# Stage orders of five engines rewritten: the first late tiles join the hand-written part, and each sort is cut in two

## The reference, cut to what matters

```
# block 1, for each of 4 batches, on layernorm(x): w1 is [512, 512], w2 is [512, 256]
def smooth_quant_linear(x, w):            # int8-like product, smoothed per column
    s  = sqrt(colmax|x| / colmax|w|)      # floors left out
    xs, ws = x / s, w * s
    x_q = round(xs / (rowmax|xs| / 127));  w_q = round(ws / (rowmax|ws| / 127))
    return x_q @ w_q.T * x_scale * w_scale.T
gate, up = split(smooth_quant_linear(x, w1));  a = silu(gate) * up
x1 = x + smooth_quant_linear(a, w2)
# block 2, on layernorm(x1): 8 experts, the best 2 of each token
weights = softmax over the best 2 of (xn @ router_w)
out = x1 + sum over the 2 experts of weight * (silu(xn @ gate_w) * (xn @ up_w)) @ down_w
```

## Time and profile before

| | us |
|---|---|
| runs of the kernel before: median (lowest to highest) | 386.32 (385.65 to 386.40) |
| the profiled execution | 386.07 |
| its span on the core | 384.2 |
| PE busy | 324.4 |
| POOL busy | 244.4 |
| DVE busy | 222.9 |
| ACT busy | 205.3 |

### The profile page before, as it was taken

How to read it: one execution, slowest core, us unless ns; L and a number is a source line. 1 busy time by engine, 2 the same in 40 slices (tenths; PEclk the granted TensorE clock), 3 DMA queues, 4 the chain that set the end, 5 groups by cost and what they waited for, 6 DMA issues and landing times.

```text
span 384.2 us, 6264 instructions
## 1 busy us (share of the span) xinstructions
PE 324.4 (84%) x1863; PEld 192.2 (50%) x1863; DVE 222.9 (58%) x511; ACT 205.3 (53%) x386; POOL 244.4 (64%) x271
## 2 busy tenths in 40 slices
PE   4697877867888876589889897999999999999980
PEld 2354535535656743385565444555555555555530
DVE  3585887889897988868577822333333333333320
ACT  1649838969987696138644333444444444444430
POOL 6484697889999961584572163556667756665441
PEclk9999989999998999989999999999999999999997
DMA  8773807654593337146344354556687666775543
GB/s 248 252 296 100 317 21 262 199 196 143 214 341 125 88 133 265 38 164 171 159 141 166 52 142 77 100 101 117 124 137 122 123 92 121 126 133 94 101 56 55
DMA packets 27552, 56.80 MB, mean 148 GB/s; under 512 B 2624, under 2 KB 13888, under 8 KB 25600
## 3 DMA queue, kind: packets, MB, share of 16 engines
q0 software_dynamic: 8736, 20.45, 29.2%
q1 hardware_dynamic: 17968, 35.39, 26.8%
q10 hardware_dynamic: 816, 0.54, 0.5%
HBM read 37.50 MB, written 18.87 MB: 147 GB/s over the span
## 4 chain that ended last, share of the span: by engine, by line
PE 45%; issue 14%; DVE 13%; POOL 13%; ACT 8%; DMA 3%; POOLq 2%; SPq 0%; DVEq 0%; ACTq 0%
PE bank_h L1306 18%; PE bank_q L1327 9%; PE bank_t L1291 3%; DVE amax L717 3%; PE bank_q L1172 3%; PE bank_q L1223 2%; DVE rmax L747 2%; ACT w_in L1027 2%; POOL out L678 2%; PE bank_h L1200 2%; DVE packed L870 2%; POOL x L639 2%; PE bank_t L1172 2%; POOL w_in L657 2%; PE bank_q L1212 2%
## 5 line engine op out<-in xcount | busy, mean ns | idle before, releaser
L1306 PE MATMUL bank_h<-gu_hi,xT 128*128 x312 | 104.0, 379 | 1.6 <-DVE xT L953 1.6
L1306 PE MATMUL bank_h<-gu_lo,xT 128*128 x156 | 59.2, 380 | 0.0
L953 DVE SCALAR_TENSOR_TENSOR xT<-bank_t,xT 128x512 f16<-128x512 f32 x39 | 26.8, 689 | 53.0 <-ACT xT L1085 53.0
L1327 PE MATMUL bank_q<-dn_hi,aT 128*128 x156 | 52.7, 380 | 3.2 <-DVE aT L971 2.9
L1306 PEld LDWEIGHTS bank_h<-gu_hi,xT 128*128 128x128 f16 x312 | 30.5, 98 | 31.0 <-issue 1.9
L657 POOL DMA_INDIRECT w_in<-tokens,gather_at x30 | 29.9, 995 | 22.8 <-PE bank_t L1291 10.8
L575 POOL TENSOR_TENSOR gu_lo<-stage,gu_hi 128x1024 bf16<-128x1024 f32 x16 | 34.0, 2135 | 9.7 <-ACT gu_hi L1042 9.5
L717 DVE TENSOR_REDUCE amax<-bank_t 128x1 f32<-128x512 f32 x48 | 30.9, 684 | 6.9 <-PE bank_t L1172 5.2
L678 POOL DMA_INDIRECT out<-h,scatter_at x17 | 26.9, 1580 | 12.1 <-ACT h L1114 5.5
L1092 ACT ACTIVATE gated<-bank_h 128x256 f32<-128x256 f32 x39 | 14.9, 383 | 36.0 <-PE bank_h L1306 33.4
L961 DVE SCALAR_TENSOR_TENSOR gated<-bank_h,gated 128x256 f32<-128x256 f32 x39 | 16.5, 422 | 30.2 <-ACT gated L1092 30.2
(11 more groups left out here) (196 smaller groups left out, 716.9 us busy)
## 6 DMA issues: line engine op xcount, KB each, us to landing
stage<-in_L_ffn_gate_proj SPq DMA_DIRECT2D x8, 512.0 KB, 4.8
stage<-in_L_ffn_up_proj SPq DMA_DIRECT2D x8, 512.0 KB, 6.2
stage<-in_L_ffn_down_proj SPq DMA_DIRECT2D x8, 512.0 KB, 5.0
x<-in_x SPq DMA_DIRECT2D x4, 1024.0 KB, 6.8
out<-x SPq DMA_DIRECT2D x4, 1024.0 KB, 4.2
tokens<-xn SPq DMA_DIRECT2D x4, 1024.0 KB, 5.4
x_in<-in_x SPq DMA_DIRECT2D x3, 1024.0 KB, 6.4
w_in<-in_fside_BxS2xS SPq DMA_DIRECT2D x3, 1024.0 KB, 5.4
```

Source lines behind the costliest of these rows:

```text
L953: dve.scalar_tensor_tensor(out=xT[i % 2][:, 1].rearrange("p c t -> p (c t)"), in0=bank, scalar=X_SCALE, in1=xT[i % 2][:, 0].rearrange("p c ...
L1306: ins = pe.matmul(bank, xT[i % 2][:, part, c], rhs[:, cols], start=(c == 0 and m == 0), stop=(c == C - 1 and m == 2))
L1327: ins = pe.matmul(bank, aT[i % 2][:, part, c], rhs[:, cols], start=(c == 0 and n == 0), stop=(c == FC - 1 and n == 2))
```

## The change

It has four parts.

1. All five lists are rewritten. They hold the same stages, apart from the new ones named below, in another order.
2. The lists in the text now reach further: `FIRST = 11`. The loop appends tiles from 11 on, and late tiles 9 and 10 stand in the lists among early tiles 6 to 9. In the lists of PE, DVE and ACT the loop's pattern is unchanged; POOL's loop still starts at tile 9 and is the same.
3. The stage `table` on PE is cut in two: `sort` runs all steps of a group but the last, `table` the last. Between them other stages may stand. For group 0 they stand next to each other; for group 1 `scores 7` is between them, for group 2 `a low 4`.
4. `FILLERS` has other numbers: 103 in place of 100. Seven now stand ahead of `rows 1 3`, seven in place of three ahead of `rows 1 1`, three ahead of `place 0`; the six ahead of `w1 transposed 1` and the five of sort step 0 are gone.

The semaphores of gathers get names of their own for early and late tiles; what they wait for is the same.

```
+FIRST = 11
-    "w1 scale row 0, high 4, normalise 1 1, high 5, silu 0, high 6, high 7, high 8, rows 1 1, rows 2 0, x up 1, "
+    "x transposed 0, high 4, high 5, normalise 1 1, silu 0, high 6, rows 1 1, high 7, rows 2 0, high 8, high 9, "
-    ("w1 columns", 0): 9, ("x columns", 0): 4, ("rows 1", 0): 2, ("w1 scale row", 0): 30, ("rows 1", 1): 3,
-    ("rows 2 inverse", 0): 18, ("w1 transposed", 1): 6, ("rows 1", 2): 6, ("product 2", 0): 8, ("sort step", 0): 5,
-    ("sort step", 1): 3, ("sort step", 2): 3, ("sort step", 3): 3,
+    ("w1 columns", 0): 9, ("x columns", 0): 4, ("rows 1", 0): 2, ("w1 scale row", 0): 28, ("rows 1", 1): 7,
+    ("rows 2 inverse", 0): 20, ("rows 1", 2): 2, ("product 2", 0): 10, ("x columns", 3): 2, ("rows 1", 3): 7,
+    ("place", 0): 3, ("sort step", 1): 3, ("sort step", 2): 3, ("sort step", 3): 3,
...
-        act_order.append(("x high", EARLY))
-        dve_order.append(("x low", EARLY))
+        act_order.append(("x high", FIRST))
+        dve_order.append(("x low", FIRST))
         for i in range(EARLY, TILES):
             if i + J < TILES:
                 pool_order.append(("gather", i + J))
...
-            if i >= EARLY + 2:
-                act_order.append(("take y", i - 2))
+        for i in range(FIRST, TILES):
+            act_order.append(("take y", i - 2))
...
+            pe_order += [("up first", i), ("a low", i - 1), ("up rest", i), ("take y", i - 1)]
+            act_order += [("a high", i - 1), ("gate", i)]
+            dve_order += [("a low", i - 1), ("up", i)]
...
-            def sort(g):
-
-                bank = ring_w.fill(pe, "table", 0, g)
+            def sort(part, g):
+
                 steps = K * len(GROUPS[g])
-                for n in range(steps):
+                bank = ring_w.fill(pe, "sort", 0, g) if part == 0 else ring_w.bank(ring_w.before("sort", 0, g))
+                for n in range(steps - 1) if part == 0 else (steps - 1,):
...
+                     "sort": partial(sort, 0), "table": partial(sort, 1),
```

44 lines of the change are left out of this document (19 added, 25 removed), and 97 rows, old and new, of tables (ACT_ORDER, DVE_ORDER, PE_ORDER, POOL_ORDER).

## The result

| | before | changed |
|---|---|---|
| median of the runs on one chip | 386.36 us (4 runs, 385.65 to 386.91) | 394.33 us (4 runs, 393.4 to 394.56) |
| ratio, 95% interval | | 1.0204 (1.0175 to 1.0232) |
| profiled execution | 386.07 us, span 384.2 | 394.46 us, span 392.6 |
| mean granted clock of PE | 0.980 | 0.966 |

What follows compares the result with a forecast made beforehand. PE was taken as the bound, its late loop already tight at 4.54 us per tile, so only the loop's start could move. Seven terms summed to -4.6 us: 381.7 us against the median, range 377.8 to 387.0.

Steps and rivals of the forecast that it cites:

- Start of batch 0: At the kernel's start, w1 transposed 0 coming first delays product 1 0 and all behind it: +0.9 us, bounds 0 and +1.3.
- Middle: Ahead of the first sort, w1 scales 3 fills a DVE wait and seven idle products cost nothing: -0.5 us.
- First sort: Group 0's sort starts some 5.5 us earlier and tile 0 fills PE's wait for residual 2: -2.0 us, bounds 0 and -2.6.
- Collision: In list 0, two of POOL's three late low stop DVE's small operations: +1.8 us, bounds 0 to +2.7.
- Rival 1: All three low stop the first sort and PE has no cover, 6.4 us: total 386.3, no change; chance 0.09.
- Clock: Newly placed idle products recover half the loss of one low-clock stretch on PE: -0.8 us, bounds -1.7 and +1.7.
- Later sorts: In groups 1 and 2, scores 7 and a low 4 fill PE's waits for the second step: -1.5 us, bounds 0 and -2.6.
- Seam: Between early and late tiles, interleaving tiles 9 and 10 cuts PE's waits of 1.4 and 1.6 us, 0.6 staying: -2.5 us.
- Rival 3: Late normalise 2 3 and token store hold gather 9: 388.6 us; chance 0.13 together with other ways to be slower.

Runs made afterwards that it cites:

- e5: Kernel before with only SP's first steps as in the change (loads of expert 3 and 4 ahead of w2 0, x again 0, x 1): 392.50 us, 1.0157.
- e1: Changed kernel with the load of expert 4 put back behind the load of x 1 on SP: 392.63 us, 1.0162.
- e8: Changed kernel with both e1's load order and e6's cut of low 21 to 23: 384.94 us, 0.9982.
- e6: Changed kernel with low 21 to 23 on 8 elements per row instead of 1024, leaving out part of one expert's weights: 388.35 us, 1.0050.
- e14: Changed kernel with 24 idle products ahead of product 1 3 on PE: 393.87 us, 1.0205.
- e11: e10 with group 1's sort also split around scores 7; computes everything: 383.34 us, 0.9926.
- e9: Kernel before up to place 2, then the changed order for the last early tiles and tiles 9 and 10, with group 2's cut: 386.36 us, 1.0023.
- e10: e9 with a low 8 ahead of up 10 on DVE and x high 10 behind a high 7 on ACT: 384.49 us, 0.9966.
- e18: Changed kernel with three repairs: e1's load order, e6's cut low and e10's two moved seam steps: 382.15 us, 0.9903.
- e16: e15 with the two seam steps moved as in e10: 391.06 us, 1.0119.
- e15: e1 with product 1 3, the last high and low steps and POOL's order around the first gathers put back as before: 394.57 us, 1.0196.
- e2: Changed kernel with high 21 to 23 moved up on ACT and low 20 ahead of gap 0 on POOL: 398.42 us, 1.0299.
- e3: Changed kernel with product 1 3 put back ahead of place 0 on DVE and PE: 404.8 us, 1.0482.
- e7: Kernel before with e6's cut of low 21 to 23: 385.25 us, 0.9974.
- e13: e1 with 24 idle products ahead of product 1 3 on PE: 392.07 us, 1.0181.

## Why the prediction was wrong, step by step

- *Start of batch 0, +0.9.* Right: `product 1 0` came at 37.28 us instead of 36.04, +1.2, inside its bounds.
- *Middle, -0.5.* This step failed, and it was the first: the term left out the order of SP's loads altogether, so it put the late load at nothing. I looked at DVE, POOL and PE there and at no row of SP. The moved load of expert 4 waits for `low 1`, the load of x 1 stands behind it, and `residual 1` came 5.9 us late. Measured alone it is +6.1 to 6.5 us in the kernel before (e5), and in the changed kernel 1.7 (e1) to 3.4 (e8 against e6), where other losses cover a part.
- *First sort, -2.0.* The start was right in size: against its mask the sort is 4.7 us earlier (5.5 forecast). In the changed kernel the gain behind it never showed, since `list 0` ate it.
- *Collision, +1.8 (0 to +2.7).* The mechanism was right, with its place; the size was not, and in the changed kernel this is the larger of the two failures. I took two `low` of three and let tile 0 cover 2.6 us. All three hit, and the cover was void: not only gather 0 but `product 1 3`, `silu 3`, the gates and `residual 2` hang behind `list 0`, so nothing that PE could do was ready. `list 0` lost 5.7 us; I had 5.3 for all three at one place and 6.4 at another. In the total it is 6.0 us (e6), and 7.7 with the load repaired (e8 against e1). Rival 1 had named "no cover", but capped it at 6.4 with nothing else lost. That most operations of `list 0` have two inputs in SBUF was misread: five of twelve do. `tile_onehot`, which I took as agreeing with that rule, is a `tensor_scalar` with one input tensor.

  The Trainium skill ("SBUF — State Buffer", "Who interferes with whom") also says of `tensor_scalar`, `copy` and `cast` that, when their operands meet its conditions, they can enter a mode that takes the ports shared with GpSimd. The three slow operations are of these kinds, with a single SBUF input, and lasted 2.04 to 2.12 us; in which mode they ran no run here shows. I had used only its line on two inputs.
- *Clock, -0.8.* The gain did not come: the mean is 0.966 against 0.980. I costed the idle products that the change places and not the pauses that it makes. What the lower clock costs by itself is not shown: e14 shows no gain from filling the largest pause, and in e6 the low stretch behind it went away with the pause.
- *Later sorts, -1.5.* The waits for `packed` fell by 1.5 us, as said: the second step of group 1 is no longer waited for, and that of group 2 for 1.1 us instead of 1.3. In time, e11 shows about 1.2 us for group 1; group 2's cut was not tested alone.
- *Seam, -2.5.* The gain did not come: as in the change, the seam is worth nothing or a loss of up to 1.8 us by its interval (e9). I took the row order of three engines together and did not follow one tile through all of them. DVE's `a low 8` behind `up 10` brought back 1.93 us. Moving two steps takes 2 to 3.5 us off each kernel (e10 against e9, e18 against e8, e16 against e15), but against the kernel before the mended seam is worth 1.1 to 1.3 us (e10, with group 2's cut in it), half of the term.
- *Rival 3* was not what held gather 9: `normalise 2 3` ended at 221.4, later than the 215.6 I named, but gather 9 was itself 10 us late and was released by `gather_at`. *Rival 1* came nearest; it missed the load.

The loop was to start 4.6 us earlier. It started 7.3 us later (`a low 10`), and gather 9 went 10.0 us later. My two signs of being wrong, a start within 1 us of the old one or waits for gathers in the late tiles, did not name this case.

## What to carry to other kernels

When an order is made anew, read the row of every queue, DMA issues first: a load that waits for a buffer holds all loads behind it. Here one early batch's input behind such a load cost 6.1 to 6.5 us (e5), and the reordering that came out best, mended seam and split sort, gave 2.3 to 2.9 (e11). Put a long GpSimd instruction beside DVE work that reads PSUM, not beside a chain of tiny ones on SBUF. And an order is good only as a whole: e2, e3 and e15 each put a step back where it stood in a faster kernel or nearer to it, and each became slower. Follow one item through all engines before moving it.

## What the hardware showed that I had not expected

- A DVE operation on 8 elements per row stands still for a whole GpSimd instruction (0.17 to 2.12 us), even with a single input tensor. One with a PSUM input ran beside the same instructions at its usual time, 1.41 and 1.61 us for two in the kernel before and in e7. In these traces it is mostly DVE that waits: GpSimd's 2.13 us per `low` stayed, but two took 4.39 us in e2 and 4.47 in e3, and one 2.43 in e3.
- The low clock can fall on other work than that right behind a pause. In e1 PE stood still for 5.84 us until 158.45, and the granted clock was 0.50 over 155 to 160 us, 0.84 over 160 to 170, and 0.50 again over 170 to 175, on tile 0. In e14 that pause was filled, the clock was 1.00 from 150 to 165 us, and it was 0.50 over 170 to 175 all the same. In e13's profiled run, which is e1 with e14's idle products, it stayed at 1.00. In all three PE had several short waits between 165 and 170 us. Executions of one kernel differ in it: e13 took 390.24 us at a mean of 0.990 and 394.38 at 0.968.
